# Unread matmuls on the tensor engine until the first input chunk lands, and the gate weights' matmuls moved into the attention loop

## The chip, the core and the metric

One core of a Trainium2 chip runs the kernel. Its engines are TensorE (PE in the profile; weight loads stand apart as PEld), VectorE (DVE), ScalarE (ACT), GpSimd (POOL) and SyncE (SP), which here only issues transfers. The metric is the device time of one execution in microseconds, as the median over runs. The profile is one further execution, and its span runs from its first to its last instruction.

## The reference

A small vision tower over 16 images. Patches are embedded, one layer of causal attention follows, and then a mixture of eight experts of which each token takes one.

```python
h = einsum('bnd,ed->bne', patches, W_proj) + b_proj + pos_emb      # 16 x 36 patches, 768 -> 256
h = concatenate([cls_tok, h], axis=1)                              # 16 x 37 = 592 tokens
h = h + attn(layernorm(h), W_qkv, b_qkv, W_out, b_out)             # 16 heads of 16, causal
x = layernorm(h)                                                   # (592, 256)
wg_n = wg / maximum(norm(wg, axis=1, keepdims=True), 1e-4)         # (8, 16)
gates = softmax((x @ w_red) @ wg_n.T)                              # which of 8 experts
idx = argmax(gates); score = gates[idx]
y = (gelu(x @ w1[e] + b1[e]) @ w2[e] + b2[e])[idx] * score         # 256 -> 1024 -> 256
out = h + y
```

All of it is float32. The kernel multiplies `w_red` and `wg_n` into one matrix `G` (256 x 8) once, so that the logits are `x @ G`.

## The kernel before

The 592 tokens are padded to 640 and lie as five tiles of 128 (`NT` = 5). Attention works on eight pairs of images (`PAIRS` = 8). Each engine has its own program, written out by hand in one block per engine. The order on an engine is the order of the code, and engines meet only at semaphores (`q[...]`), so an instruction behind a wait stands until the wait is over.

**Embedding.** SP issues six chunks of the input, 448 KB each (L289), then `pos` (L290), `wqkv` and the rest. TensorE multiplies chunk by chunk: the first three chunks for all five tiles each (L455 to L458), then, with the last three loaded, tile by tile, and each finished tile raises `embedded` (L472 to L475). A float32 matmul stands in the trace as two records, so the 30 embedding matmuls are 60 records on L452.

**Gate weights.** Behind chunk 0 stands a small transposition of the normalised `wg` (L461, into PSUM bank `BZ` = 7) and behind chunk 1 two small matmuls, four records, that make `G` (L466). VectorE normalises `wg` before (L719 to L724) and copies both results out of PSUM (L734, L736). Before the first `turn_normalised`, TensorE waits for `g_ready` (L528).

**First layernorm.** VectorE adds the bias into `pos` (L744, five operations), then for each tile adds the embedding from PSUM (L750), takes the statistics (L726 to L728) and, when GpSimd has the inverse root (L945), writes the normalised tile `xn` into `hz` (L731). TensorE turns each tile (`turn_normalised`, L482), ScalarE copies it out (L358), and values (L494) and keys and queries (L501) follow in an order written out at L530 to L552. GpSimd also adds `bout` into `h` tile by tile (L956).

**Attention loop.** Step `i` (L592) holds the scores of pair `i`, the turned output of pair `i - 3`, the transposed probabilities of pair `i - 1`, and the attention output of pair `i - 2`. VectorE has the maximum and the shift of the scores (L772, L776), ScalarE the exponential (L381) and copies. From step 4 on, projection (L620), second layernorm, `zt` (L605) and logits (L610, the first reader of `G`) of a token tile come in at `PROJ_AT`. Banks are shared: `keys_or_queries(1, 2)`, the third of the second half's four, writes bank 7, which VectorE empties with L766, and that raises `q0_ready` to 2.

**Experts.** Routing on VectorE from 89.7 us, gathers by GpSimd, then eight tiles of expert matmuls (L666, L678).

Of the kernel before, what the change touches and what calls it, by code (L numbers as in the profile page):

```python
# [12 lines left out]
BF16 = mybir.dt.bfloat16  # L13
# [7 lines left out]
P = 128  # L21
# [5 lines left out]
KD = D // P  # L27
# [15 lines left out]
E, F = 8, 1024  # L43
# [2 lines left out]
OVF = (T + E * (P - 1)) // P - E  # L46
RING = 4
EPS = 1e-5
FAR = 4096.0
NOROW = 1024  # L50

# [61 lines left out]
def vit_tower(nc, embed_in, places_in, b_proj, w_qkv, b_qk, b_v, w_out, b_out, wg, w_red_t, w1, b1, w2, b2,  # L113
              cf_d, cb_d, iota_d, out):
    ctx = ExitStack()
    with ctx:
        def sb(name, shape, dt=F32):
            return ctx.enter_context(nc.sbuf_tensor(name, shape, dt))
# [18 lines left out]
        ident = C("ident")  # L137
# [16 lines left out]
        wgn = sb("wgn", [E, 16])  # L154
        wgv = sb("wgv", [E, 4])
        wgnt = sb("wgnt", [16, E])
        wredt = sb("wredt", [16, D])
        G = sb("G", [P, KD, E])
# [25 lines left out]
        hz = sb("hz", [P, NT, 2 * D])  # L184

        xn = hz[:, :, D:2 * D]
        zt = sb("zt", [P, 2, KD, P])

        lg = sb("lg", [P, NT, E])
# [41 lines left out]
        def late(n):  # L231
# [16 lines left out]
        ps = ctx.enter_context(nc.psum_tensor("ps", [P, 8, 512], F32))  # L248
# [3 lines left out]
        BP, BO, BZ = 4, 6, 7  # L252
# [8 lines left out]
            loaded_bv loaded_bout loaded_b1 loaded_b2 loaded_wg loaded_wred  # L261
            embedded h_saved veps_ready rstd_ready xn_ready xnt_ps xnt_ready vrow_ps vrow_ready vrow_stored
            wg_sq wg_norm wgn_ready wgnt_ps wgnt_ready g_ps g_ready bqs_ready
            qk_ps k0_ready k1_ready q0_ready q1_ready v_zeroed v_ready pads_ready
            scores_ps shifted_ready probs_ready probst_ps probst_ready o_ps o_ready ot_ps ot_ready
            hb_ready proj_ps veps2_ready rstd2_ready h2_ready z_ready zt_ps zt_ready logits_ps
            hz_stored hot_ready low_ready elow_ready cum_ps info_ready place_ready info_ps slots_ready
# [3 lines left out]
        q = {n: sem(n) for n in names}  # L271
# [177 lines left out]
        def _(pe):  # L449

            def embed(k, j):
                return nc.tensor.matmul(ps[:, j, 0:D], emb[:, k, j * P:(j + 1) * P], emb[:, k, TP:TP + D],  # L452
                                        start=(k == 0), stop=(k == KE - 1))

            for k in range(KE - 3):  # L455
                pe.wait_ge(loaded_emb[k], 16)
                for j in range(NT):
                    embed(k, j)  # L458
                if k == 0:
                    pe.wait_ge(q["wgn_ready"], 1)  # L460
                    nc.tensor.transpose(ps[0:16, BZ, 0:E], wgn[:, :], ident[0:E, 0:E]).then_inc(q["wgnt_ps"], 1)  # L461
                if k == 1:
                    pe.wait_ge(q["wgnt_ready"], 1)
                    pe.wait_ge(q["loaded_wred"], 16)
                    for c in range(KD):
                        m = nc.tensor.matmul(ps[:, BZ, 16 + c * E:16 + (c + 1) * E], wredt[:, c * P:(c + 1) * P],  # L466
                                             wgnt[:, :], start=True, stop=True)
                    m.then_inc(q["g_ps"], 1)

            for k in range(KE - 3, KE):  # L470
                pe.wait_ge(loaded_emb[k], 16)
            for j in range(NT):  # L472
                for k in range(KE - 3, KE):
                    m = embed(k, j)
# [50 lines left out]
                                             start=False, stop=(c == KD - 1), tile_position=(r * ROW_B, a * ROW_B))  # L525
                m.then_inc(q["scores_ps"], 1)

            pe.wait_ge(q["g_ready"], 1)  # L528
            pe.wait_ge(q["loaded_wqkv"], 16)
            turn_normalised(0)  # L530
            turn_normalised(1)
# [53 lines left out]
            def turned(u):  # L585
# [3 lines left out]
                                            o[:, u % 2, c * P:(c + 1) * P], ident[0:ROWS, 0:ROWS])  # L589
                m.then_inc(q["ot_ps"], 1)  # L590

            for i in range(1, STEPS):  # L592
                if i < PAIRS:
                    scores(i)
                if 0 <= i - 3 < PAIRS:
                    turned(i - 3)
                if 0 <= i - 1 < PAIRS:
                    transposed(i - 1)
                if 0 <= i - 2 < PAIRS:
                    attend(i - 2)  # L600
                if i - 1 in PROJ_AT:
                    j = PROJ_AT[i - 1]
                    pe.wait_ge(q["z_ready"], j + 1)
                    for k in range(KD):
                        m = nc.tensor.transpose(ps[:, BZ, k * P:(k + 1) * P],  # L605
                                                hz[:, j, D + k * P:D + (k + 1) * P], ident)
                    m.then_inc(q["zt_ps"], 1)
                    pe.wait_ge(q["zt_ready"], j + 1)
                    for k in range(KD):
                        m = nc.tensor.matmul(lgp[:, j, :], zt[:, j % 2, k, :], G[:, k, :],  # L610
                                             start=(k == 0), stop=(k == KD - 1))
                    m.then_inc(q["logits_ps"], 1)
                if i in PROJ_AT:
                    j = PROJ_AT[i]
                    if j == 0:
                        pe.wait_ge(q["loaded_wout"], 16)
                        pe.wait_ge(q["q0_ready"], 2)
                    pe.wait_ge(q["ot_ready"], KD * (i - 2))
                    for k in range(KD):
                        m = nc.tensor.matmul(ps[:, BZ, 0:D], ot[:, k, j * P:(j + 1) * P], wout[:, k, :],  # L620
                                             start=(k == 0), stop=(k == KD - 1))
                    m.then_inc(q["proj_ps"], 1)
# [4 lines left out]
            for i in range(NT - 1):  # L627
                m = nc.tensor.matmul(cum[:, i + 1:NT, :], CB("ones"),
                                     hotb[:, i, :].unsqueeze(1).to_broadcast([P, NT - 1 - i, E]),
                                     start=False, stop=(i == NT - 2))  # L630
# [75 lines left out]
        def _(dve):  # L706
# [7 lines left out]

            V = nc.vector

            dve.wait_ge(q["loaded_cf"], 16)
            dve.wait_ge(q["loaded_wg"], 16)
            link(V.tensor_tensor(wgsq[:, :], wgs[:, :], wgs[:, :], ALU.mult))  # L719
# [10 lines left out]
            def norm_apply(dst, src, m, rs, j):  # L730
                return V.tensor_scalar(dst, src, m[:, j, 0:1], rs[:, j:j + 1], ALU.subtract, ALU.mult)  # L731

            dve.wait_ge(q["wgnt_ps"], 1)
            V.tensor_copy(wgnt[:, :], ps[0:16, BZ, 0:E]).then_inc(q["wgnt_ready"], 1)  # L734
            dve.wait_ge(q["g_ps"], 1)
            V.tensor_copy(G[:, :, :], ps[:, BZ, 16:16 + KD * E].rearrange("p (k e) -> p k e", e=E))\  # L736
                .then_inc(q["g_ready"], 1)
            dve.wait_ge(q["loaded_bqk"], 16)
            V.tensor_scalar(bkm[:, :], C("kmask"), bqk[:, KD + 1:KD + 2], None, ALU.mult)
            V.tensor_scalar(bqs[:, :], bqk[:, 0:KD], DH ** -0.5, None, ALU.mult).then_inc(q["bqs_ready"], 1)  # L740
# [40 lines left out]
            first_keys_and_queries(0)  # L781
            softmax_top(0)
            first_keys_and_queries(1)
            for i in range(1, STEPS):
                if i < PAIRS:
                    softmax_top(i)
                if i - 1 in PROJ_AT:
                    j = PROJ_AT[i - 1]
                    dve.wait_ge(q["proj_ps"], j + 1)
                    dve.wait_ge(q["hb_ready"], j + 1)  # L790
                    V.tensor_tensor(hz[:, j, 0:D], ps[:, BZ, 0:D], h[:, j, :], ALU.add).then_inc(q["h2_ready"], 1)
                    dve.wait_ge(q["h2_ready"], j + 1)
                    norm_stats(hz[:, j, 0:D], stats2, mv2, veps2, j, q["veps2_ready"])
                if 0 <= i - 2 < PAIRS:

                    u = i - 2
                    o3 = ps[0:ROWS, BO, 0:VI].rearrange("p (h w) -> p h w", w=VW)
                    dve.wait_ge(q["o_ps"], u + 1)
                    link(V.reciprocal(rsum[:, u % 2, :], o3[:, :, DH:VW].rearrange("p h w -> p (h w)")))
                    if u >= 2:  # L800
                        dve.wait_ge(q["ot_ps"], u - 1)
                    V.tensor_tensor(o[:, u % 2, :].rearrange("p (h w) -> p h w", w=DH), o3[:, :, 0:DH],
                                    rsum[:, u % 2, :].unsqueeze(2).to_broadcast([ROWS, HEADS, DH]), ALU.mult)\
                        .then_inc(q["o_ready"], 1)
                if i - 1 in PROJ_AT:
                    j = PROJ_AT[i - 1]
                    dve.wait_ge(q["rstd2_ready"], j + 1)
                    norm_apply(hz[:, j, D:2 * D], hz[:, j, 0:D], mv2, rstd2, j).then_inc(q["z_ready"], 1)
# [239 lines left out]
```

## Time and profile before

| | |
|---|---|
| time, median of 3 runs | 171.74 us (170.84 to 173.59) |
| the profiled execution's own time | 170.72 us |
| its span | 168.8 us |
| mean granted TensorE clock over the span | 0.875 |
| PE busy | 132.3 us (78%), 1027 records |
| PEld busy | 112.3 us (67%) |
| DVE busy | 66.4 us (39%) |
| ACT busy | 46.5 us (28%) |
| POOL busy | 39.1 us (23%) |
| HBM read, written | 27.34 MB, 3.01 MB |

The page gives busy shares by engine. The chain of waits goes back from the last instruction to what released each, and so shows the work that sets the end. The timeline shows instructions in order, with the idle time of their engine before them and what ended it. In the windows view each stretch has busy times and the granted clock of TensorE as a share of 2.4 GHz, so 0.50 is 1.2 GHz.

### The profile page before, as it was taken

The numbers are of one execution on the slowest core, as the hardware profiler recorded it, in microseconds if no ns is written. First come the engines' busy times: TensorE is split into PE (matmuls) and PEld (weight loads), VectorE is DVE, ScalarE is ACT, GpSimd is POOL, SyncE is SP. The second block draws the span as 40 slices with busy tenths as digits, with TensorE's granted clock in tenths as the row PEclk, the third lists the DMA queues.
The fourth block names the chain that finished last, engine by engine and source line by source line (L and its number), as shares of the span: only waits on it lengthen the run. The fifth ranks groups of instructions, "written<-read, shape, count | busy, mean of one in ns | idle before, by whom it ended". The sixth has DMA issues, their size and how long they took to land.

```text
span 168.8 us, 2667 instructions
## 1 busy us (share of the span) xinstructions
PE 132.3 (78%) x1027; PEld 112.3 (67%) x1027; DVE 66.4 (39%) x192; ACT 46.5 (28%) x130; POOL 39.1 (23%) x49
## 2 busy tenths in 40 slices
PE   0999997998993985946733127899999999999960
PEld 0788775775782864834502026899999999999850
DVE  0217989377765462142036862242121221212130
ACT  1100135376652441221000000750523315042200
POOL 8200475045091001010010054000422404012022
PEclk9999999999999597595555555999999999999998
DMA  5999925929999943930100024101999998700000
GB/s 186 302 371 396 372 73 157 179 54 187 202 367 364 373 152 113 386 112 11 62 36 26 4 62 134 54 0 18 344 321 375 298 370 318 275 19 0 21 22 26
DMA packets 18622, 30.13 MB, mean 178 GB/s; under 512 B 2455, under 2 KB 13848, under 8 KB 18478
## 3 DMA queue, kind: packets, MB, share of 16 engines
q1 hardware_dynamic: 16958, 26.93, 49.8%
q0 software_dynamic: 1024, 2.71, 4.7%
q10 hardware_dynamic: 624, 0.29, 0.9%
q8 instruction: 10, 0.16, 0.4%
q14 instruction: 6, 0.05, 0.1%
HBM read 27.34 MB, written 3.01 MB: 180 GB/s over the span
## 4 chain that ended last, share of the span: by engine, by line
PE 62%; DVE 17%; DMA 8%; issue 5%; POOL 3%; ACT 2%; SPq 2%; POOLq 0%; DVEq 0%
PE ps L666 18%; PE ps L678 16%; DMA pos<-places 6%; PE ps L620 5%; DVE hz L731 4%; PE ps L501 4%; PE ps L581 3%; PE ps L522 3%; PE ps L610 3%; PE ps L563 3%; DMA early<-hz_scratch,growu 2%; DVE stats L726 2%; PE ps L605 2%; SPq L289 2%; DVE negmax L772 1%
## 5 line engine op out<-in xcount | busy, mean ns | idle before, releaser
L666 PEld LDWEIGHTS ps<-early,w1s 128*128 128x128 f32 x256 | 31.1, 200 | 2.2 <-issue 1.9
L666 PE MATMUL ps<-early,w1s 128*128 128x128 f32 x256 | 31.4, 283 | 1.3 <-DVE early L895 1.3
L678 PE MATMUL ps<-w2s,early 128*128 128x256 f32 x128 | 28.8, 379 | 0.0
L435 ACT ACTIVATE early<-ps,b1s 128x128 f32<-128x128 f32 x64 | 18.2, 370 | 31.5 <-PE ps L666 31.5
L678 PEld LDWEIGHTS ps<-w2s,early 128*128 128x128 f32 x128 | 23.8, 190 | 2.9
L977 POOL DMA_INDIRECT out<-early,srowu x8 | 8.0, 1006 | 48.4 <-DVE early L908 48.4
L452 PE MATMUL ps<-early 128*128 128x256 f32 x60 | 15.3, 414 | 3.9 <-DMA early<-embed_in 3.9
L452 PEld LDWEIGHTS ps<-early 128*128 128x128 f32 x60 | 12.2, 209 | 5.8 <-DMA early<-embed_in 3.9
L903 DVE TENSOR_TENSOR ysum<-ps,b2s 128x256 f32<-128x256 f32 x8 | 3.4, 424 | 26.8 <-PE ps L678 26.8
L895 DVE COPY early<-ps 128x256 f32<-128x256 f32 x8 | 3.4, 424 | 22.0 <-PE ps L654 22.0
L972 POOL DMA_INDIRECT early<-hz_scratch,growu x8 | 8.1, 1010 | 14.6 <-DVE growu L860 12.8
L968 POOL TENSOR_TENSOR rstd<-veps,cf 128x1 f32<-128x1 f32 x5 | 2.7, 548 | 33.8 <-DVE veps L728 33.8
L605 PE MATMUL ps<-cf,hz 128*128 128x128 f32 x10 | 2.7, 359 | 10.0 <-DVE hz L731 10.0
L772 DVE TENSOR_REDUCE negmax<-ps 101x16 f32<-101x592 f32 x8 | 6.2, 775 | 10.4 <-PE ps L522 10.3
L402 ACT ACTIVATE ot<-ps,bv 128x74 f32<-128x74 f32 x16 | 4.3, 320 | 17.1 <-PE ps L588 17.1
L605 PEld LDWEIGHTS ps<-cf,hz 128*128 128x128 f32 x10 | 1.2, 166 | 11.3 <-DVE hz L731 11.3
L501 PE MATMUL ps<-xnt,wqkv 128*128 128x296 f32 x32 | 8.6, 416 | 0.0
L581 PEld LDWEIGHTS ps<-vbd,probst 111*64 111x64 f32 (+1 forms) x192 | 7.0, 139 | 2.2 <-issue 2.0
L620 PE MATMUL ps<-wout,ot 128*128 128x256 f32 x20 | 8.4, 564 | 0.0
L581 PE MATMUL ps<-vbd,probst 111*64 111x51 f32 (+2 forms) x192 | 7.7, 229 | 0.9 <-issue 0.7
L563 PE MATMUL ps<-cf,probs 101*111 101x101 f32 x48 | 7.3, 297 | 0.8 <-ACT probs L381 0.8
L638 PE MATMUL ps<-info,wide 128*128 128x6 bf16 x40 | 1.4, 168 | 7.6 <-DVE info L850 3.9
(122 smaller groups left out, 171.6 us busy)
## 6 DMA issues: line engine op xcount, KB each, us to landing
w1s<-w SPq DMA_DIRECT2D x8, 1024.0 KB, 5.6
w2s<-w SPq DMA_DIRECT2D x8, 1024.0 KB, 9.5
early<-embed_in SPq DMA_DIRECT2D x6, 448.0 KB, 6.7
hz_scratch<-hz SPq DMA_DIRECT2D x5, 256.0 KB, 2.0
b2s<-b SPq DMA_DIRECT2D x1, 1024.0 KB, 11.8
wqkv<-w_qkv SPq DMA_DIRECT2D x1, 768.0 KB, 11.5
w1s<-v_scratch SPq DMA_DIRECT2D x3, 256.0 KB
w2s<-v_scratch SPq DMA_DIRECT2D x3, 256.0 KB
```

The lines of the kernel that those rows point to most:

```text
L435: nc.scalar.activation(gt[:, t % 2, f, :], ps[:, 2 * (t % 2) + f // 4, (f % 4) * P:(f % 4 + 1) * P], ACT.Gelu, bias=b1t[:, f:f + 1]).then_ ...
L452: return nc.tensor.matmul(ps[:, j, 0:D], emb[:, k, j * P:(j + 1) * P], emb[:, k, TP:TP + D], start=(k == 0), stop=(k == KE - 1))
L501: m = nc.tensor.matmul(ps[:, QK_BANK[a][n], 0:HALF], wqkv[:, k, col:col + P], xnt[:, k, a * HALF:(a + 1) * HALF], start=(k == 0), stop=(k ...
L563: m = nc.tensor.transpose(ps[0:GS, BP + half, g * ROWS:(g + 1) * ROWS], probs[:, u % 2, at:at + GS], ident[0:ROWS, 0:ROWS])
L581: m = nc.tensor.matmul(ps[a * ROW_B:a * ROW_B + w, BO, g * GH * VW:g * GH * VW + n], probst[:, u % 2, at:at + w], vbd[:, col:col + n], sta ...
L605: m = nc.tensor.transpose(ps[:, BZ, k * P:(k + 1) * P], hz[:, j, D + k * P:D + (k + 1) * P], ident)
L620: m = nc.tensor.matmul(ps[:, BZ, 0:D], ot[:, k, j * P:(j + 1) * P], wout[:, k, :], start=(k == 0), stop=(k == KD - 1))
L666: m = nc.tensor.matmul(ps[:, 2 * (t % 2) + f // 4, (f % 4) * P:(f % 4 + 1) * P], w1s[:, r, k, f * P:(f + 1) * P], xt[:, t % 2, k, :], star ...
L678: m = nc.tensor.matmul(ps[:, 4 + t % 2, 0:D], gt[:, t % 2, f, :], w2s[:, r, f, :], start=(f == 0), stop=(f == FT - 1))
L772: link(V.tensor_reduce(negmax[:, u % 2, :].rearrange("p (r h) -> p r h", r=2), s3, AX.X, ALU.max, negate=True))
L972: pool.indirect_dma_start(rows[:, t % RING, :], None, hz_d, bass.IndirectOffsetOnAxis(growu[:, t:t + 1], 0)).then_inc(gathered[t % RING], 16)
L977: pool.indirect_dma_start(out, bass.IndirectOffsetOnAxis(srowu[:, t:t + 1], 0), yout[:, t % 2, :], None, bounds_check=T - 1, oob_is_err=Fa ...
```

## The change

Three edits.

1. VectorE's first instruction is now a fill of `blank` with zeros, a bfloat16 view of the first 256 columns of `hz`. TensorE waits for it and issues six matmuls of 128x128 by 128x512 bfloat16 from it into bank 7. Nobody reads what they write. The embedding starts behind them.
2. The gate weights' transposition and matmuls, their two copies on VectorE and the wait for `g_ready` leave the embedding. The transposition now stands in front of the attention loop, behind a new wait for `q0_ready` = 2 (bank 7 must have been emptied). The two matmuls stand in step 1 behind `transposed(0)`.
3. VectorE copies `wgnt` in front of its own loop and `G` in step 2, behind `softmax_top(2)`. TensorE waits for `g_ready` at the first projection.

```diff
+WARM, WARM_N = 6, 512
...
+        blank = hz[:, 0, 0:WARM_N // 2].bitcast(BF16)
...
+            pe.wait_ge(q["blank_ready"], 1)
+            for _ in range(WARM):
+                nc.tensor.matmul(ps[:, BZ, 0:WARM_N], blank[:, 0:P], blank, start=True, stop=True)
             for k in range(KE - 3):
                 pe.wait_ge(loaded_emb[k], 16)
                 for j in range(NT):
                     embed(k, j)
-                if k == 0:
-                    pe.wait_ge(q["wgn_ready"], 1)
-                    nc.tensor.transpose(ps[0:16, BZ, 0:E], wgn[:, :], ident[0:E, 0:E]).then_inc(q["wgnt_ps"], 1)
-                if k == 1:
-                    pe.wait_ge(q["wgnt_ready"], 1)
-                    pe.wait_ge(q["loaded_wred"], 16)
-                    for c in range(KD):
-                        m = nc.tensor.matmul(ps[:, BZ, 16 + c * E:16 + (c + 1) * E], wredt[:, c * P:(c + 1) * P],
-                                             wgnt[:, :], start=True, stop=True)
-                    m.then_inc(q["g_ps"], 1)
...
-            pe.wait_ge(q["g_ready"], 1)
             pe.wait_ge(q["loaded_wqkv"], 16)
...
+            def gate_weights():
+                pe.wait_ge(q["wgnt_ready"], 1)
+                pe.wait_ge(q["loaded_wred"], 16)
+                for c in range(KD):
+                    m = nc.tensor.matmul(ps[:, BZ, 16 + c * E:16 + (c + 1) * E], wredt[:, c * P:(c + 1) * P],
+                                         wgnt[:, :], start=True, stop=True)
+                m.then_inc(q["g_ps"], 1)
+
+            pe.wait_ge(q["q0_ready"], 2)
+            pe.wait_ge(q["wgn_ready"], 1)
+            nc.tensor.transpose(ps[0:16, BZ, 0:E], wgn[:, :], ident[0:E, 0:E]).then_inc(q["wgnt_ps"], 1)
             for i in range(1, STEPS):
...
                     attend(i - 2)
+                if i == 1:
+                    gate_weights()
...
+                    if j == 0:
+                        pe.wait_ge(q["g_ready"], 1)
...
+            V.memset(blank, 0.0).then_inc(q["blank_ready"], 1)
             dve.wait_ge(q["loaded_cf"], 16)
...
-            dve.wait_ge(q["wgnt_ps"], 1)
-            V.tensor_copy(wgnt[:, :], ps[0:16, BZ, 0:E]).then_inc(q["wgnt_ready"], 1)
-            dve.wait_ge(q["g_ps"], 1)
-            V.tensor_copy(G[:, :, :], ps[:, BZ, 16:16 + KD * E].rearrange("p (k e) -> p k e", e=E))\
-                .then_inc(q["g_ready"], 1)
...
             first_keys_and_queries(1)
+            dve.wait_ge(q["wgnt_ps"], 1)
+            V.tensor_copy(wgnt[:, :], ps[0:16, BZ, 0:E]).then_inc(q["wgnt_ready"], 1)
             for i in range(1, STEPS):
                 if i < PAIRS:
                     softmax_top(i)
+                if i == 2:
+                    dve.wait_ge(q["g_ps"], 1)
+                    V.tensor_copy(G[:, :, :], ps[:, BZ, 16:16 + KD * E].rearrange("p (k e) -> p k e", e=E))\
+                        .then_inc(q["g_ready"], 1)
```

TensorE at the start of the program, before. The names are those of the code, the line numbers those of the kernel in question, and `early` is the buffer that holds the embedding's input.

```order
L448 UNCONDITIONAL_BRANCH
L452 MATMUL ps<-early 128x256 x5
L461 MATMUL ps<-cf,wgn 16x8
L452 MATMUL ps<-early 128x256 x5
L466 MATMUL ps<-wgnt,wredt 128x8 x2
L452 MATMUL ps<-early 128x256 x20
L482 MATMUL ps<-cf,hz 128x128 x4
```

The same place in the changed kernel, where the embedding is L454 and the turning L477.

```order
L450 UNCONDITIONAL_BRANCH
L459 MATMUL ps<-hz 128x512 x6
L454 MATMUL ps<-early 128x256 x30
L477 MATMUL ps<-cf,hz 128x128 x4
L489 MATMUL ps<-wqkv,xnt 128x256 x2
L477 MATMUL ps<-cf,hz 128x128 x2
```

Six matmuls stand in front of the embedding, and its 30 now follow each other without the two gate pieces.

TensorE from the second half's keys and queries (L501) to the scores of pair 2 (second L516), before.

```order
L501 MATMUL ps<-xnt,wqkv 128x296 x8
L516 MATMUL ps<-cb 101x296 x2
L522 MATMUL ps<-wide,qt 64x148
L522 MATMUL ps<-wide,qt 37x148 x2
L522 MATMUL ps<-wide,qt 64x148 x2
L522 MATMUL ps<-wide,qt 37x148 x2
L522 MATMUL ps<-wide,qt 64x148
L563 MATMUL ps<-cf,probs 111x101 x6
L516 MATMUL ps<-cb 101x296 x2
```

The same place in the changed kernel.

```order
L496 MATMUL ps<-xnt,wqkv 128x296 x8
L596 MATMUL ps<-cf,wgn 16x8
L511 MATMUL ps<-cb 101x296 x2
L517 MATMUL ps<-wide,qt 64x148
L517 MATMUL ps<-wide,qt 37x148 x2
L517 MATMUL ps<-wide,qt 64x148 x2
L517 MATMUL ps<-wide,qt 37x148 x2
L517 MATMUL ps<-wide,qt 64x148
L557 MATMUL ps<-cf,probs 111x101 x6
L590 MATMUL ps<-wgnt,wredt 128x8 x2
L511 MATMUL ps<-cb 101x296 x2
```

The transposition stands in front of the scores of pair 1, and the two gate matmuls stand between the transposed probabilities of pair 0 and the scores of pair 2.

VectorE from the second half's keys (L761) to the first pair's output, before.

```order
L761 TENSOR_SCALAR wide<-ps,bqk,cf 128x8x37 x4
L766 TENSOR_SCALAR qt<-ps,bqs 128x296
L772 TENSOR_REDUCE negmax<-ps 101x16
L776 TENSOR_TENSOR probs<-ps,negmax 101x592
L772 TENSOR_REDUCE negmax<-ps 101x16
L776 TENSOR_TENSOR probs<-ps,negmax 101x592
L799 RECIPROCAL rsum<-ps 101x16
```

The same place in the changed kernel.

```order
L766 TENSOR_SCALAR wide<-ps,bqk,cf 128x8x37 x4
L771 TENSOR_SCALAR qt<-ps,bqs 128x296
L790 COPY wgnt<-ps 16x8
L777 TENSOR_REDUCE negmax<-ps 101x16
L781 TENSOR_TENSOR probs<-ps,negmax 101x592
L777 TENSOR_REDUCE negmax<-ps 101x16
L781 TENSOR_TENSOR probs<-ps,negmax 101x592
L796 COPY G<-ps 128x16
L810 RECIPROCAL rsum<-ps 101x16
```

The copy of `wgnt` stands in front of the softmax of pair 1, and the copy of `G` behind that of pair 2.

## Rows read from the trace of the kernel before

**Rows 1.** Chain of waits, 0 to 40 us: start us, us, work.

```profile
3.69 10.07 DMA pos<-places
...
32.14 4.18 PE ps L501 x16
36.32 0.25 PE ps L516 x2
...
37.31 0.79 DVE negmax L772
```

**Rows 2.** Timeline of DVE: start us, us, engine, line, operation, [idle before, releaser].

```profile
13.85 2.07 DVE L744 SCALAR_TENSOR_TENSOR pos<-bproj,cf,pos 128x256 f32<-128x256 f32 x5 [2.37 <-DMA pos<-places]
15.83 0.42 DVE L750 TENSOR_TENSOR h<-ps,pos 128x256 f32<-128x256 f32 x1
...
18.25 0.40 DVE L731 TENSOR_SCALAR hz<-h,mv,rstd 128x256 f32<-128x256 f32 x1
...
21.61 0.42 DVE L750 TENSOR_TENSOR h<-ps,pos 128x256 f32<-128x256 f32 x1
...
23.66 3.35 DVE L731 TENSOR_SCALAR hz<-h,mv,rstd 128x256 f32<-128x256 f32 x1 [0.44 <-POOL rstd L945]
```

**Rows 3.** Timeline of PE, 0 to 30 us.

```profile
3.94 3.95 PE L452 MATMUL ps<-early 128*128 128x256 f32 x10 [3.94 <-DMA early<-embed_in]
7.82 0.17 PE L461 MATMUL ps<-cf,wgn 8*16 8x8 f32 x1
7.92 2.42 PE L452 MATMUL ps<-early 128*128 128x256 f32 x10
10.28 0.61 PE L466 MATMUL ps<-wgnt,wredt 16*128 16x8 f32 x4
10.81 8.90 PE L452 MATMUL ps<-early 128*128 128x256 f32 x40
19.55 0.38 PE L482 MATMUL ps<-cf,hz 128*128 128x128 f32 x2
20.23 0.44 PE L482 MATMUL ps<-cf,hz 128*128 128x128 f32 x2 [0.30 <-DVE hz L731]
...
21.75 0.44 PE L482 MATMUL ps<-cf,hz 128*128 128x128 f32 x2 [0.21 <-DVE hz L731]
...
27.06 0.44 PE L482 MATMUL ps<-cf,hz 128*128 128x128 f32 x2 [0.93 <-DVE hz L731]
```

**Rows 4.** Timeline of POOL, 0 to 30 us.

```profile
1.12 3.73 POOL L939 MEMSET vbd<- 111x4352 f32 x1
```

**Rows 5.** Timeline of all engines, 35 to 40.5 us.

```profile
35.68 0.52 DVE L766 TENSOR_SCALAR qt<-ps,bqs 128x296 f32<-128x296 f32 x1
...
36.16 0.42 PE L516 MATMUL ps<-cb 128*101 128x296 bf16 x2
...
38.18 0.73 PE L522 MATMUL ps<-wide,qt 64*64 64x148 f32 x16
...
38.98 0.78 DVE L772 TENSOR_REDUCE negmax<-ps 101x16 f32<-101x592 f32 x1
...
39.67 0.83 PE L563 MATMUL ps<-cf,probs 101*111 101x101 f32 x6 [0.76 <-ACT probs L381]
```

**Rows 6.** Timeline of DVE, then of PE, 26 to 54 us.

```profile
41.36 0.26 DVE L799 RECIPROCAL rsum<-ps 101x16 f32<-101x16 f32 x1 [0.79 <-PE ps L581]
...
53.05 0.44 PE L605 MATMUL ps<-cf,hz 128*128 128x128 f32 x2 [2.14 <-DVE hz L731]
```

**Rows 7.** Windows: stretch, us, busy (records) PE, PEld, DVE, ACT, POOL, granted clock, DMA.

```profile
54.00:55.00 1.00, 1.00 (x10) 0.78 (x14) 0.00 (x0) 0.00 (x0) 0.00 (x0) 0.92 0.98 393
...
58.00:59.00 1.00, 1.00 (x23) 0.97 (x21) 0.17 (x1) 0.75 (x2) 0.00 (x0) 0.87 1.08 347
```

**Rows 8.** Chain of waits, projections at either level of the clock.

```profile
47.09 1.06 PE ps L620 x4
...
83.09 1.92 PE ps L620 x4
```

More of the change, by code:

```diff
@@ L263, in vit_tower @@
             wg_sq wg_norm wgn_ready wgnt_ps wgnt_ready g_ps g_ready bqs_ready
-            qk_ps k0_ready k1_ready q0_ready q1_ready v_zeroed v_ready pads_ready
+            qk_ps k0_ready k1_ready q0_ready q1_ready v_zeroed v_ready pads_ready blank_ready
             scores_ps shifted_ready probs_ready probst_ps probst_ready o_ps o_ready ot_ps ot_ready
```

## The prediction

> **What bounds the kernel now.** I read the chain of waits first, since the page's 78% of PE says only that TensorE is busy, not where its work sets the end. From 3.69 us the chain stands on the transfer of `pos` for 10.07 us, to 13.76 us [rows 1]. Then it is VectorE's: five `pos` operations from 13.85 us, the first one released by that transfer after 2.37 us of idle, the first `h` at 15.83 us, the fifth at 21.61 us, that is one tile each (21.61 - 15.83) / 4 = 1.45 us [rows 2]. The last `xn` begins at 23.66 us and takes 3.35 us, where the same operation took 0.40 us at 18.25 us; TensorE, idle for 0.93 us, is released by it at 27.06 us [rows 2, 3]. The reader is to see that no embedding matmul and no gate matmul stands in this part. Only behind 27.06 us is TensorE the bound: sixteen records of keys and queries from 32.14 us for 4.18 us, then the scores of pair 1 at 36.32 us, and their maximum at 37.31 us [rows 1].
>
> How far off the path is the embedding? The forty records from 10.81 us lead to the next one at 19.55 us: 8.74 / 40 = 0.2185 us each [rows 3]. The first tile needs 24 records fewer than the last, so it is complete about 19.55 - 24 x 0.2185 = 14.3 us, and VectorE takes it at 15.83 us: 1.5 us of slack. The fifth is complete at about 19.7 us and taken at 21.61 us [rows 2, 3]. Behind the embedding TensorE turns tile 0 at 19.55 us, but the order of its program puts the turning of tile 1 next, and that waits for VectorE until 20.23 us; the turning of tile 2 waits until 21.75 us [rows 3]. So an earlier embedding has nothing to hand on.
>
> **Edit 1, six unread matmuls.** The first ten records took 7.82 - 3.94 = 3.88 us against 10 x 0.2185 = 2.19 us later [rows 3]: 1.7 us is what the low clock costs in this trace. Their mean pace is 0.39 us, and half the later speed would be 0.437 us, so about eight of the ten ran at the 1.2 GHz level. Six bfloat16 matmuls of 512 columns are not in the trace. With 0.39 us or twice that for each, the six take 2.3 to 4.7 us. I take 2.6 us, because 512 one-pass columns are nearest to a record that streams its 256 twice. Starting at about 0.9 us, as GpSimd's own fills begin before 1.12 us [rows 4], they end at about 3.5 us, inside the 3.94 us that TensorE idles anyway [rows 3]. At the upper bound they end at 5.6 us, and the embedding starts 1.7 us late, which is what it then saves at the high clock. Gain on the path: 0 either way, covered by the wait for `pos`. If the clock is high from the first record, the embedding ends at about 3.94 + 60 x 0.2185 = 17.05 us, 2.5 us earlier than now, and TensorE then idles until `xn` of tile 0 at 18.65 us.
>
> In the Trainium skill, TensorE: Matmul & The Clock Gate, Part 1, "What's actually happening", says that the throttled state is the default and activity releases it, and the block behind it puts the ramp at under 1% of a typical kernel's span. By that the most there is to win would be 1.7 us of 168.8 us, and 172.1 - 1.7 = 170.4 us would follow if all of it were on the path; the rows put it off the path, so the sum by them is 0.
>
> **Edit 2, out of the embedding.** Removed there are one record at 7.82 us, for which TensorE needs from 7.82 to 10.28 us less ten records, 2.46 - 2.19 = 0.27 us, and four at 10.28 us, 0.53 us [rows 3]. That is 0.8 us of TensorE, off the path for the same reason. VectorE's two copies stood in front of its wait for `pos`, so they were free.
>
> **Edit 2, in front of the loop.** This one is on the path. The transposition stands between the keys and queries and the scores of pair 1. Its new wait is for the `qt` operation that begins at 35.68 us and ends at 36.20 us; until now the scores' first record began at 36.16 us, with its weights loaded ahead [rows 5]. So the wait itself costs 0.05 to 0.15 us, since a signal needs about 0.07 us from an end to the next start (38.18 + 0.73 = 38.91 to 38.98 us) [rows 5]. The transposition costs 0.10 us (7.82 to 7.92 us) at least and 0.27 us with the broken pace of its neighbours [rows 3]. Bounds: 0.10 and 0.42 us. I take 0.35 us, near the upper one, because the wait also keeps the scores' weight loads from being drawn ahead. Behind the waiting transposition stand the scores of pair 1, and for these VectorE waits. All that follows moves by that.
>
> **Edit 2, in step 1.** The four gate records stand in front of the scores of pair 2. They cost 0.53 us, or 0.73 us with as much again for the pace as above (0.20). The work that hides them is an idle stretch: TensorE finishes pair 2's scores at 38.91 us and stands until 39.67 us, 0.76 us, for ScalarE's exponential of pair 1, which does not depend on pair 2 [rows 5]. What is late next is the maximum of pair 2, at 38.98 us with no idle before it. With 0.73 us more it begins at 39.7 us, shift and maximum end about 41.3 us. Without the idle stretch the full 0.5 to 0.7 us would be on the path.
>
> **Edit 3, the copies.** That of `wgnt` lands in the idle before 37.31 us. That of `G`, 0.17 us at the most, comes behind the shift of pair 2, so VectorE is free at about 41.5 us, where it now starts the reciprocal at 41.36 us after 0.79 us of idle [rows 6]. It may be 0.1 us late; TensorE's other work stands between that and its use. I count 0. The wait for `g_ready` at the first projection (47.09 us [rows 8]) is long over.
>
> **Sum.** 168.8 + 0 + 0 + 0.35 = 169.15 us of span; with the 170.72 - 168.8 = 1.92 us around it, 171.07 us. The median of the runs shown is 1.02 us above the profiled one, so 171.74 + 0.35 = 172.1 us.
>
> **Rivals.**
>
> *The clock falls again at about 20 us.* With an embedding that ends at 17.05 us, TensorE idles 1.6 us, turns tile 0, and idles 1.1 us more to 20.23 us. In this trace the clock fell at 54.9 us after an idle stretch of 2.14 us and came back at 58.25 us, 3.4 us later (0.92 and 0.87 are shares of a second) [rows 6, 7]; after 0.93 us of idle at 27.06 us it stayed. The new stretches lie between. Such a fall halves 3.4 us of work, so 1.7 us is lost, less the 0.93 + 0.21 us that TensorE waits there now [rows 3]: +0.55 us. If it stays low twice as long, 3.4 - 1.15 = +2.3 us. Time: 172.1 + 0.55 = 172.7, up to 174.4 us. It decides if the embedding ends before about 18 us.
>
> *The early part comes back.* All of 1.7 + 0.8 us off TensorE's front would give 171.74 + 0.35 - 2.5 = 169.6 us. It needs an execution in which the embedding, not `pos`, comes last. That holds from the point where tile 0 is complete after 15.83 us, which takes 1.5 us more of low clock loss than here. Against it stands the 10.07 us of `pos` in the chain [rows 1]; in executions whose clock rises later than in this one, some tenths may come back, hence 171.4 to 171.8 us.
>
> *Later stages change level.* A projection on the chain takes 1.06 us at the high clock and 1.92 us at the low one [rows 8], and the executions before spread over 2.75 us. A shift by tenths may move which of them runs at which level: two of them more or fewer, 1.7 us, so 170.4 or 173.8 us. Nothing in the change steers it.
>
> *The fill waits for GpSimd.* If VectorE's fill is held up by the 3.73 us fill of `vbd` that ends at 4.85 us [rows 4], as the 3.35 us operation was held beside GpSimd's adds [rows 2], the unread matmuls end at 4.85 + 2.6 = 7.5 us and the embedding starts 3.5 us late. At the high clock tile 0 is complete at 7.5 + 36 x 0.2185 = 15.4 us, in time; with a low start (1.7 us) at 17.1 us, 1.3 us late: 173.4 us. The Trainium skill, SBUF — State Buffer, "Who interferes with whom", lists copy, cast and tensor_scalar as what takes the port pair shared with GpSimd, and names a fill for another chip generation only. No row here shows a fill beside a fill.
>
> **Chances.** Forecast, all hidden but 0.2 to 0.45 us: 0.45. The wait and transposition hidden too, or some tenths back in front (171.4 to 171.8 us): 0.15. Clock falls near 20 us: 0.2. Early part comes back in full: 0.05. Other levels later: 0.1, half on each side. Fill waits: 0.05. The range of 170.4 to 173.6 us leaves out the full early gain, the doubled low stretch and half of the later levels' upper end, together under 0.2. A measurement of this kernel can tell about 2%, 3.4 us, from no change. Faster by that would need 168.3 us, which only the early part plus lucky levels give: 0.04. Slower needs 175.2 us: 0.04. Within: 0.92.
>
> **What would show it.** Right: `pos` still ends the wait on VectorE at about 13.8 us and TensorE is released at about 27.1 us by the last `xn`; the embedding ends before 18.7 us; the scores' first record begins at about 36.5 us; TensorE's idle before the second transposed probabilities shrinks from 0.76 us to under 0.25 us, while they begin at about 40.0 us. Wrong: VectorE's first `h` earlier than 15.8 us, or a first `h` later because the fill came late; a granted clock of 0.50 between 19 and 28 us; idle before the second transposed probabilities that is gone with their start after 40.2 us.

## The result: 1.8% slower in the first comparison, 0.2% in all executions

| | before | changed |
|---|---|---|
| first comparison, median | 172.67 us (4 executions, 170.84 to 173.87) | 174.53 us (4 executions, 174.19 to 184.07) |
| ratio | | 1.018, 95% interval 1.010 to 1.026 |
| all executions of the study, median | 173.84 us (61, 170.52 to 176.10) | 174.21 us (10, 172.22 to 184.07) |
| profiled execution, time and span | 170.72, 168.8 us | 174.19, 172.3 us |
| mean granted clock of the profiled execution | 0.875 | 0.852 |

The forecast was 172.1 us in a range of 170.4 to 173.6 us, and 174.53 us lies outside. The first comparison rests on few executions of a kernel whose own times spread over 5.6 us; its ratio uses only executions within 1.5% of each kernel's fastest, which here cuts through one continuous spread. Over all executions the medians differ by 174.21 - 173.84 = 0.37 us. Resampling them gives -0.3 to +1.8 us for that difference, so the times alone do not tell it from none.

The rows of the changed kernel that answer to [rows 2] and [rows 4] come from its timelines of DVE and POOL (start us, us, engine, line, operation, idle before).

```profile
0.85 0.27 DVE L726 MEMSET hz<- 128x256 uint32 x1 [0.85 <-PEq L1053]
...
14.85 2.07 DVE L749 SCALAR_TENSOR_TENSOR pos<-bproj,cf,pos 128x256 f32<-128x256 f32 x5 [3.25 <-DMA pos<-places]
16.83 0.41 DVE L755 TENSOR_TENSOR h<-ps,pos 128x256 f32<-128x256 f32 x1
...
24.66 3.35 DVE L741 TENSOR_SCALAR hz<-h,mv,rstd 128x256 f32<-128x256 f32 x1 [0.44 <-POOL rstd L956]
...
1.12 3.73 POOL L950 MEMSET vbd<- 111x4352 f32 x1
```

The fill ran beside GpSimd's short ones, took 0.27 us and was over when the long one began. `pos` still ends VectorE's wait and the last `xn` still takes 3.35 us, both exactly 1.00 us later than before, with everything between them.

The timeline of PE of the changed kernel, which answers to [rows 3] and [rows 5]:

```profile
1.18 2.74 PE L459 MATMUL ps<-hz 128*128 128x512 bf16 x6 [1.18 <-DVE hz L726]
3.87 3.03 PE L454 MATMUL ps<-early 128*128 128x256 f32 x10
7.58 4.58 PE L454 MATMUL ps<-early 128*128 128x256 f32 x20 [0.69 <-DMA early<-embed_in]
13.27 6.71 PE L454 MATMUL ps<-early 128*128 128x256 f32 x30 [1.10 <-DMA early<-embed_in]
19.82 0.39 PE L477 MATMUL ps<-cf,hz 128*128 128x128 f32 x2
21.23 0.44 PE L477 MATMUL ps<-cf,hz 128*128 128x128 f32 x2 [1.02 <-DVE hz L741]
...
28.07 0.44 PE L477 MATMUL ps<-cf,hz 128*128 128x128 f32 x2 [0.94 <-DVE hz L741]
...
37.26 0.17 PE L596 MATMUL ps<-cf,wgn 8*16 8x8 f32 x1
37.36 0.46 PE L511 MATMUL ps<-cb 128*101 128x296 bf16 x2
...
39.17 0.61 PE L590 MATMUL ps<-wgnt,wredt 16*128 16x8 f32 x4
...
40.10 0.73 PE L517 MATMUL ps<-wide,qt 64*64 64x148 f32 x16
40.92 0.83 PE L557 MATMUL ps<-cf,probs 101*111 101x101 f32 x6
```

The six unread matmuls fit in front of the first chunk. The embedding now waits twice for its chunks and is done at 19.8 us, not at 17 us. The gate matmuls at 39.17 us take the idle time before the second transposed probabilities, which is 0.09 us now (40.83 to 40.92 us) where it was 0.76 us.

The two chains of waits where they part for good, the kernel before first (start us, us, work):

```profile
72.62 0.87 PE ps L581 x18
...
74.61 0.45 PE ps L605 x2
...
103.06 5.23 PE ps L666 x32
```

```profile
73.86 1.47 PE ps L575 x18
...
76.44 0.70 PE ps L612 x2
...
105.25 6.52 PE ps L675 x32
```

The same instructions stand on the same path and take longer, because TensorE ran at the low clock: the granted clock from 73.86 to 75.33 us of the changed kernel is 0.50, and from 72.6 to 73.5 us of the kernel before it is 1.00. Followed along the chain, the spans' 172.3 - 168.8 = 3.5 us are: `pos` 1.00 us, the transposition 0.24 us, the low clock at 73.9 and 76.4 us 0.60 + 0.25 = 0.85 us, the gather and small pieces 0.09 us, and the low clock in the first expert 1.29 us. Only 0.24 us stands where the change made an edit.

### The profile page after: what moved, and what is told of

Same layout as the page of the kernel before. It is cut to its first block, busy times and chain, and to the rows that moved or that the text cites. A ratio compares the mean times of both kernels' runs of the same rounds, so it can differ in the third digit from the quotient of the medians.

```text
span 172.3 us, 2682 instructions
## 1 busy us (share of the span) xinstructions
PE 136.5 (79%) x1033; PEld 114.2 (66%) x1033; DVE 66.6 (39%) x193; ACT 46.7 (27%) x130; POOL 39.1 (23%) x49
## 4 chain that ended last, share of the span: by engine, by line
PE 62%; DVE 17%; DMA 8%; issue 5%; POOL 2%; SPq 2%; ACT 2%; POOLq 0%; DVEq 0%
PE ps L675 18%; PE ps L687 16%; DMA pos<-places 6%; PE ps L629 5%; PE ps L575 4%; DVE hz L741 4%; PE ps L496 4%; PE ps L517 3%; PE ps L617 3%; PE ps L557 2%; DMA early<-hz_scratch,growu 2%; DVE stats L736 2%; PE ps L612 2%; SPq L291 2%; DVE negmax L777 1%
## 5 line engine op out<-in xcount | busy, mean ns | idle before, releaser
L675 PEld LDWEIGHTS ps<-early,w1s 128*128 128x128 f32 x256 | 32.4, 206 | 2.2 <-issue 1.9
L675 PE MATMUL ps<-early,w1s 128*128 128x128 f32 x256 | 32.7, 290 | 1.3 <-DVE early L906 1.3
L454 PE MATMUL ps<-early 128*128 128x256 f32 x60 | 14.3, 395 | 1.8 <-DMA early<-embed_in 1.8
L454 PEld LDWEIGHTS ps<-early 128*128 128x128 f32 x60 | 11.6, 199 | 4.9 <-DMA early<-embed_in 1.9
L575 PEld LDWEIGHTS ps<-vbd,probst 111*64 111x64 f32 (+1 forms) x192 | 7.8, 151 | 2.3 <-issue 2.2
L575 PE MATMUL ps<-vbd,probst 111*64 111x51 f32 (+2 forms) x192 | 8.5, 243 | 1.0 <-issue 0.7
```

The costliest lines, as they stand in the source:

```text
L575: m = nc.tensor.matmul(ps[a * ROW_B:a * ROW_B + w, BO, g * GH * VW:g * GH * VW + n], probst[:, u % 2, at:at + w], vbd[:, col:col + n], sta ...
L675: m = nc.tensor.matmul(ps[:, 2 * (t % 2) + f // 4, (f % 4) * P:(f % 4 + 1) * P], w1s[:, r, k, f * P:(f + 1) * P], xt[:, t % 2, k, :], star ...
```

## The experiments

**Both kernels again, and each half of the change alone.** The question was which of the four large terms (`pos`, the transposition, the low clock in the projections and in the first expert) come with the change. The first two runs have no edit. The third leaves the unread matmuls and the fill out of the changed kernel, the fourth adds them to the kernel before.

```diff
# third run, against the changed kernel
-            pe.wait_ge(q["blank_ready"], 1)
-            for _ in range(WARM):
-                nc.tensor.matmul(ps[:, BZ, 0:WARM_N], blank[:, 0:P], blank, start=True, stop=True)
...
-            V.memset(blank, 0.0).then_inc(q["blank_ready"], 1)
# fourth run, against the kernel before
+            pe.wait_ge(q["blank_ready"], 1)
+            for _ in range(WARM):
+                nc.tensor.matmul(ps[:, BZ, 0:WARM_N], blank[:, 0:P], blank, start=True, stop=True)
...
+            V.memset(blank, 0.0).then_inc(q["blank_ready"], 1)
```

> The kernel before, unchanged, as the yardstick for how much the arrival of pos and the clock's levels differ between executions. If the 3.5 us between the two profiles are mostly executions that differ (theory A), this one has a pos landing anywhere from 13.7 to 15 us, clock changes at other times than the first profile, and a ratio of 1.000 with an interval of about 1%. If the changed kernel causes them (theory B), this profile repeats the first: pos at 13.76 us, fall at 54.9, rise at 106.1 us, span 168.8 us.

> The changed kernel, unchanged. Theory A (direct cost 0.25 us, the rest executions that differ): ratio about 1.002 to 1.006. Theory B (the change itself causes a later pos or worse clock levels): ratio 1.015 to 1.02 again, pos landing near 14.75 us again, chain pieces of the first expert at the low clock again.

> Only the gate weights' matmuls are moved, no unread matmuls and no fill. Theory A: +0.25 us (ratio 1.0015). Theory B with the unread matmuls as the cause: also about 1.0015. Theory C (the 1.25 us by which the loop is shifted, or the gate's place, drives stages into the low clock): 1.008 or more.

> Only the fill and the six unread matmuls, the gate matmuls stay in the embedding. Theory A: 1.000. Theory B with the unread matmuls as the cause: 1.010 to 1.018, with pos landing about 1 us later. Theory C: 1.000.

On one chip, beside 11 executions of the kernel before with a median of 174.07 us (170.52 to 175.57):

| run | median us (6 executions) | first `pos` operation us | from it to the maximum of pair 1 us | clock at 0.50 in the profile, 50 to 160 us |
|---|---|---|---|---|
| kernel before, first profile | | 13.85 | 23.46 | 54.8 to 58.3, 65.1 to 71.9, 75.3 to 106.0 |
| changed, first profile | | 14.85 | 23.70 | 56.3 to 59.7, 66.6 to 110.9 |
| a1, kernel before | 173.53 | 14.00 | 23.45 | 54.9 to 61.7, 68.5 to 71.9, 75.4 to 109.5 |
| a2, changed | 173.94 | 13.94 | 23.70 | 54.7 to 64.9, 68.3 to 75.2, 78.6 to 109.3 |
| a3, gate move only | 173.35 | 13.94 | 23.70 | 54.7 to 61.5, 68.3 to 109.3 |
| a4, unread matmuls only | 173.79 | 13.97 | 23.47 | 54.0 to 64.2, 67.6 to 74.5, 77.9 to 112.0 |

The kernel before, measured against itself, has a ratio of 1.011, interval 1.000 to 1.021: as much as each of the others (1.009, 1.012, 1.013). So theory A holds for the clock: the change costs 0.24 us on the path, and the levels behind 54 us differ between executions of one kernel. Of the 1.00 us of `pos` the four runs say only that none of them repeats it. The fourth column is the change's cost on the path and repeats to 0.01 us: 23.70 us with the gate move, 23.46 us without, whatever the unread matmuls do. The rise of the clock in the first expert came at 106.0 us in one profile of the kernel before and at 109.5 us in the next, a1. There the chain shows the first expert of the unchanged kernel, longer than the 6.52 us of the changed one:

```profile
103.44 6.69 PE ps L666 x32
```

What the unread matmuls did to the first half of the embedding is seen in the timelines of PE of a2, with them, and then of a3, without them.

```profile
3.92 8.20 PE L454 MATMUL ps<-early 128*128 128x256 f32 x30
...
4.01 8.15 PE L454 MATMUL ps<-early 128*128 128x256 f32 x30 [4.01 <-DMA early<-embed_in]
```

At the later pace the 30 records would take 30 x 0.2185 = 6.6 us. Both runs needed 1.6 us more, nearly all of it the low clock, so here the unread matmuls saved none of it. (The windows view reads 1.00 before the first change of the clock that a trace records, so the low clock at the start is read from the pace of the matmuls.)

The executions point the same way. Those 57 of the kernel before that have a mean granted clock on record, grouped by it:

| mean granted clock | times, us |
|---|---|
| 0.875 | 170.52, 170.62 |
| 0.865 to 0.867 | 171.91 to 172.53 (5 executions) |
| 0.857 to 0.861 | 172.12 to 173.84 (12) |
| 0.849 to 0.852 | 173.06 to 176.10 (16) |
| 0.840 to 0.844 | 174.44 to 175.84 (22) |

The executions of the changed kernel lie in or near these rows: 0.866 with 172.22 us, 0.852 to 0.858 with 173.59 to 174.83 us (six; the one of 174.23 us at 0.857 is 0.4 us above its row), 0.841 with 175.60 and 175.61 us. Its tenth took 184.07 us at 0.762. A straight line of time against the microseconds at the low level leaves 12% of the variance of the 57 and single executions up to 1.9 us off, so the clock is most of the spread and not all of it. The same line through 78 executions of these four kernels, without the one of 184.07 us and with one offset for each kernel, gives the whole change 0.48 us, standard error 0.17, the gate move alone -0.27 and the unread matmuls alone 0.06, both with a standard error of 0.20. That is the limit of what the times tell; the 0.24 us is from the traces.

The granted clock in 40 slices of the span (tenths of full speed), from the page, for a1 and for a2:

```profile
PEclk9999999999999579685555555699999999999996
```

```profile
PEclk9999999999998558576555555799999999999998
```

Up to slice 13, some 55 us, both are high. Behind it they mix in another order each time.

**Does `pos` bound the front?** SP was made to wait for `pos` before it issues `wqkv` and the rest: on the kernel before, on the changed kernel, and on the kernel before with the unread matmuls.

```diff
+            sp.wait_ge(q["loaded_pos"], 16)
             sp.dma_start(wqkv[:, :, :], w_qkv.rearrange("(k p) n -> p k n", p=P)).then_inc(q["loaded_wqkv"], 16)
```

> The kernel before, but SP waits for the arrival of pos before it issues wqkv and what follows. Tests the step that pos, not the embedding, bounds the front. If right, pos lands 2 to 3 us earlier (it shares the transfer engines with 3.2 MB less), and the first h moves from 15.9 us to where the embedding of tile 0 is complete, about 14.5 us: -1.0 to -1.5 us on everything behind. If the embedding bounded the front already, nothing moves.

> The changed kernel with the same wait for pos on SP. If the unread matmuls are worth nothing only because pos comes last, they and the gate's absence are worth something here: the embedding of tile 0 is complete near 12 to 13 us, so the first h lies 1 to 2 us before that of the same edit on the kernel before; the maximum of pair 1 lies 23.7 us behind it instead of 23.46 us. If the unread matmuls do not help at all, the first h lies 0.8 us earlier at most (the gate's matmuls).

> The wait for pos on SP and the unread matmuls, gate matmuls left in the embedding. First h within 0.8 us of the run with both edits, and no 0.24 us in front of the scores of pair 1: net about equal to or up to 0.5 us behind the run with the whole change.

Medians of 12 executions (one of b1 took 239 us): 172.54, 172.76 and 172.40 us, beside 173.98 us of the kernel before (29 executions). The intervals of all three ratios take in 1. The first `pos` operation began at 13.73, 14.12 and 13.84 us, so the transfers behind `pos` do not slow it and the expectation failed there. That of b2 failed too: its first `h` came at 16.11 us, behind the 15.72 us of b1, where 1 to 2 us earlier was expected. Something else moved: the last `xn` no longer took 3.35 us. POOL in the kernel before, then POOL and DVE in b1:

```profile
23.58 0.63 POOL L949 COPY vbd<-cf 111x256 f32<-111x256 f32 x1
24.09 2.76 POOL L956 TENSOR_TENSOR h<-h,bout 128x256 f32<-128x256 f32 x4
```

```profile
23.48 0.63 POOL L950 COPY vbd<-cf 111x256 f32<-111x256 f32 x1
25.70 2.78 POOL L957 TENSOR_TENSOR h<-h,bout 128x256 f32<-128x256 f32 x4 [1.60 <-DMA bout<-b_out]
...
23.55 0.70 DVE L732 TENSOR_SCALAR hz<-h,mv,rstd 128x256 f32<-128x256 f32 x1 [0.44 <-POOL rstd L946]
```

`bout` came later with the rest, so GpSimd's four adds did not stand right behind its copy, and VectorE was held for the copy alone. So the 3.35 us of [rows 2] were GpSimd's hold. From the first `pos` operation to the maximum of pair 1 the three need 22.88, 22.55 and 22.37 us: 0.6 to 1.2 us less. In b1 the clock rose only at 9.1 us and TensorE itself was behind (it turned tiles 0 and 1 in one go from 20.44 us), and b3 with the unread matmuls needs 22.88 - 22.37 = 0.5 us less. That is one execution of each; c2 and c4 below, which differ in the same edit, need the same time. In b3 another cost shows: with the gate matmuls left in the embedding, the transposition behind chunk 0 held TensorE for 1.79 us, until `wgn` was there at 8.3 us.

**Is it the clock behind 54 us?** The fourth run of that job keeps TensorE busy with unread matmuls where it waits in the projections and in the routing.

```diff
+KEEP_Z = (16, 16, 8, 16, 16)
+KEEP_R = (6, 14, 13, 3)
...
+            def keep(n, bank, cols):
+                for _ in range(n):
+                    nc.tensor.matmul(ps[:, bank, 0:cols], CB("before"), cb[:, 0:cols], start=True, stop=True)
...
+                    pe.wait_ge(q["h2_ready"], j + 1)
+                    keep(KEEP_Z[j], BZ, 208)
                     pe.wait_ge(q["z_ready"], j + 1)
...
+            keep(KEEP_R[0], 0, 512)
             pe.wait_ge(q["hot_ready"], 1)
...
+            keep(KEEP_R[1], 0, 512)
             pe.wait_ge(q["info_ready"], 1)
...
+                if part:
+                    keep(KEEP_R[2], 0, 512)
                 pe.wait_ge(q["place_ready"], part + 1)
...
+            keep(KEEP_R[3], 0, 512)
             turn_rows(0)
```

> The kernel before with unread bfloat16 matmuls while TensorE waits in the projections (16, 16, 8, 16, 16 of 208 columns behind h2_ready) and in the routing (6, 14, 13 and 3 of 512 columns). Tests whether the clock's levels behind 54 us make the spread of executions. If so, the granted clock stays at 1.00 from the first rise on, the executions agree within 1 us instead of 5 us, and the time falls by 3.5 to 6 us (1.5 us for each projection, 1.5 us and more at the first expert). If the levels are a mere by-product, the time grows by what the unread matmuls cost, 0 to 3 us, and the spread stays.

164.03 us (161.62 to 165.46, six executions) beside 173.98 us: ratio 0.947, interval 0.931 to 0.963. That is more than expected, and the spread is 3.8 us, less than before but not under 1 us. The rest of the spread again goes with the clock: 161.62 us at a mean of 0.994, 165.46 us at 0.959. The timeline of PE in the profiled one, at the second projection, and the chain at the first expert:

```profile
61.58 1.60 PE L455 MATMUL ps<-cb 128*128 128x208 bf16 x16 [0.20 <-DVE hz L804]
63.52 0.44 PE L613 MATMUL ps<-cf,hz 128*128 128x128 f32 x2 [0.34 <-DVE hz L744]
```

```profile
96.22 6.72 PE ps L678 x32
```

The wait of 2.14 us in front of the turned tile is down to 0.20 and 0.34 us, and the work behind it starts no later. But in this execution the clock was still low from 78.4 to 81.8 us, and again from 95.5 us, just ahead of the first expert, whose 32 records took 6.72 us.

**The change where the clock is kept, and the adds put later.** Four runs on one chip. c1 is the changed kernel with the counts of b4. The other three have slightly more unread matmuls, three of them in front of the first expert, and put GpSimd's copy and adds behind the last `xn`: on the kernel before (c2), on the changed kernel (c3), and on the kernel before with the six unread matmuls in front (c4).

```diff
-KEEP_Z = (16, 16, 8, 16, 16)
-KEEP_R = (6, 14, 13, 3)
+KEEP_Z = (18, 18, 8, 18, 18)
+KEEP_R = (7, 16, 16, 4)
...
             turn_rows(0)
+            keep(3, 0, 512)
             hidden(0)
...
+            pool.wait_ge(q["xn_ready"], NT)
             pool.wait_ge(q["v_zeroed"], 1)
```

> The whole change with the unread matmuls in projections and routing of b4_clock_kept, same counts. If the change costs 0.25 us on the path and all else between the two kernels was the clock's levels, the first maximum of pair 1 lies 0.24 us further behind the first h than in b4 (21.48 us there) and the median is 164.0 + 0.25 us, within 0.7 us. If the change also steers later stages into the low clock, 165.5 us or more even here.

> The kernel before, GpSimd's copy into vbd and its adds of bout put behind the last xn, and slightly more unread matmuls (18, 18, 8, 18, 18; 7, 16, 16, 4 and 3 in front of the first expert). The 3.35 us of the last xn should fall to 0.40 us and TensorE should turn tile 4 at about 26.1 us, when its own work ends, instead of 27.1 us: -0.9 us. With fewer low stretches another 0 to 2 us. Median 161 to 163.5 us. If the 3.35 us are VectorE's own, they stay.

> The same two edits on the changed kernel. Here TensorE's queue behind the embedding is close to the bound, so an earlier embedding can be worth up to 0.5 us in executions whose clock rises late, against 0.24 us of the transposition: within 0.5 us of c2. If the unread matmuls paid their 1.7 us, 1 us or more below c2.

> The same two edits with the fill and the six unread matmuls only, gate matmuls left in the embedding. Without the 0.24 us of the transposition it should be the fastest of the three by 0 to 0.4 us, if the change's cost is that transposition.

| run | median us | executions | from the first `pos` operation to the maximum of pair 1 us |
|---|---|---|---|
| kernel before, same chip | 173.54 | 11, 171.98 to 175.88 | |
| c1, change, clock kept | 162.21 | 7, 161.49 to 166.63 | 23.69 (b4: 23.47) |
| c2, adds late | 160.24 | 6, 159.77 to 160.46 and one of 792.34 | 22.31 |
| c3, change, adds late | 160.26 | 6, 160.05 to 161.93 | 22.55 |
| c4, unread matmuls in front, adds late | 161.01 | 6, 159.83 to 163.49 | 22.30 |

c2 has a ratio of 0.928 to the kernel before (interval 0.924 to 0.932), 13.3 us less, below the 161 to 163.5 us that were expected. About 1.2 us of it belong to the adds put later (23.46 - 22.31 us on the path), so the unread matmuls in the waits are worth about 12 us here, an estimate, and 173.98 - 164.03 = 10 us in b4, where they stand alone. Five of the six executions agree within 0.7 us; nothing on record explains the sixth, at a mean clock of 1.000. With the clock high all through, the whole change costs 0.02 us in the medians of c3 and c2 and 0.24 us on the path. c1 shows the expected step (23.69 - 23.47 = 0.22 us), but its median missed the expected 164.25 us by 2.0 us, on the fast side, nearer to b4's fastest than to b4's median. c4 did not come out fastest as expected: its median is 0.8 us above that of c2. Its traced step is that of c2, but its first `pos` operation began at 14.79 us for 13.90 us in c2, and one of its executions had a mean clock of 0.971 and 163.49 us.

PE's clock by slices in c2, then its DVE row of the last `xn`, and the chain at the first expert:

```profile
PEclk9999999999999999999999999999999999999999
```

```profile
23.70 0.41 DVE L745 TENSOR_SCALAR hz<-h,mv,rstd 128x256 f32<-128x256 f32 x1 [0.44 <-POOL rstd L959]
```

```profile
93.92 3.81 PE ps L678 x32
```

The last `xn` is back at 0.41 us from 3.35 us, and the first expert at 3.81 us from 5.23 and 6.52 us.

## Why the prediction was wrong, point by point

**What bounds the front** was right. `pos`, not the embedding, ends VectorE's wait in both kernels, the path to 27 us is VectorE's, and taking 0.8 us of gate matmuls off TensorE's front brought nothing. One figure in it was off, and with it the sign "before 18.7 us": the embedding did not end at 17.05 us but at 19.8 us, and at 18.9 us in a2. It did not start at the high clock, which rose only at 5.1 us in the one and at 6.9 us in the other (7.0 us in the kernel before, 6.9 us in a3), and it waits for the chunks (0.69 and 1.10 us of idle in the profile above). I had counted only TensorE's own pace, which in [rows 3] never waits behind its first chunk.

**The unread matmuls** took 2.74 us from 1.18 us, for the 2.6 us taken from 0.9 us. They ended at 3.9 us, with nothing to spare and nothing lost. What they were to give, 1.7 us on TensorE, came only in part: over the eight profiles with them the clock rose between 4.2 and 7.0 us, over the six without between 6.7 and 9.1 us.

**The transposition in front of the loop** was forecast at 0.35 us in bounds of 0.10 and 0.42 us and measured 0.24 us (23.69 to 23.70 us in four traces with it, 23.45 to 23.47 us in four without; 22.55 and 22.31 us in c3 and c2). The rows give its parts: with the 1.00 us of `pos` taken off, the wait puts the first record from 36.16 to 36.26 us, 0.10 us; the transposition takes 0.10 us more (37.26 to 37.36 us); and the two records behind it take 0.46 us for 0.42 us. The term was taken too near its upper bound: the neighbours kept their pace but for 0.04 us. **The gate matmuls in step 1** were hidden as worked out: the maximum of pair 2 lies 2.35 us behind that of pair 1 where it lay 1.67 us, 0.68 us for a forecast of 0.73 us, and the second transposed probabilities did not move beyond the 0.24 us.

**The step that failed is the one from the trace's time to the median.** "So 171.74 + 0.35 = 172.1 us" took a median of three executions for the kernel's level. Over 61 executions it is 173.84 us, and drawing three at random gives a median of 171.74 us or less in about 1 of 80 draws. With 173.84 + 0.24 the same sum would have been 174.1 us, for a measured 174.21 us over ten executions and 174.53 us over the first four.

**The rival "later stages change level"** was the right mechanism with the wrong size. I priced two projections, 1.7 us, gave it 0.1, and let the range end at 173.6 us. Between the two profiles it made 0.85 + 1.29 = 2.1 us, and over the executions of the kernel before, 170.5 to 176.1 us, it goes with 88% of the variance. I left out the first expert: [rows 8] price a projection, and 32 records at 5.23 against 3.81 us price the expert. That the profiled execution had a mean clock of 0.875 and stood at the fast end of 2.75 us of spread among three was in front of me.

**The other rivals.** The clock did not fall near 20 us in any trace; in the changed kernel the idle stretch that it needed was not there, since the embedding ended late. (The 0.92 and 0.87 in that rival are shares of a microsecond, not of a second.) The fill did not wait for GpSimd: it was over at 1.12 us, when the long fill began, so whether the long one would have held it was not tried. The Trainium skill, SBUF — State Buffer, "Who interferes with whom", says that of a VectorE operation in a two-port form and a GpSimd operation the later one is blocked for the whole of the other. That agrees with 3.35 us against 0.41 us once GpSimd's work was moved; which form the VectorE operation had, no run here shows.

**One thing stays open.** The first `pos` operation began at 14.70 us or later in three of the eight profiles with unread matmuls in front (first profile of the change, c1, c4) and in none of the six without; the others lie between 13.73 and 14.12 us. In those three the transfer of `pos` began 0.2 to 0.8 us later than in the kernel before, but so it did in b2 (4.28 us), where the operation began at 14.12 us. If the unread matmuls had no part in it, three late ones would all fall among the eight with a chance of 0.15. Whether that is chance or the unread matmuls was not settled; the times at equal clock give the unread matmuls alone 0.06 us, standard error 0.20.

## What to carry to other kernels

Before a forecast of tenths, look at how wide the kernel's own executions lie and what goes with it; here they go with the mean granted clock, and a median of three says less than the step that is forecast. Work put in front of the first input pays only if the work behind it is what comes last; look which transfer releases the path. Unread matmuls were worth most where TensorE waits again and again in the middle of the kernel: 10 us in b4, against nothing measurable at its start.

## What the runs showed of the hardware

- A waiting TensorE costs twice. Between 54 and 111 us its longest waits are 2.1 to 3.9 us, and it is at 1.2 GHz for 42 us of the span in the fastest execution of the kernel before and for 55 us in one of 175.14 us (worked out from mean clocks of 0.875 and 0.841 and spans of 168.7 and 173.3 us). The same instructions take 0.45 or 0.70 us, 3.81 or up to 6.72 us. With unread matmuls in these waits the granted clock stayed at 1.00 up to the end of the span (c2).
- When the level changes is not tied to the program: unchanged code had its last rise at 106.0 us in one execution and at 109.5 us in the next, with the work at the same place to 0.4 us.
- An operation of 0.40 us on VectorE took 3.35 us when it began 0.08 us behind a GpSimd copy with four adds right behind that, and 0.70 us behind the copy alone. The hold passed from one GpSimd instruction to the next without VectorE getting in.
